# Relative-position rows of 800 bytes in a decoder layer's self-attention, their constant end filled on chip, and 72 queries turned in every tile

## The chip, the cores and the metric

One core of one Trainium2 chip runs the whole program in one launch. The metric is device time in microseconds (us).

## What is computed

A decoder layer in float32 on x of 4 x 1024 x 256: self-attention with relative positions, cross-attention to a context of 4 x 154 x 256, and a gated feed-forward with quantised activations and weights, each followed by a residual sum and a layer norm. The change is in the self-attention, with 16 heads of 16:

```python
attn = jnp.einsum('bhld,bhrd->bhlr', q, k) * scale
dist = jnp.clip(jnp.arange(L)[None, :] - jnp.arange(L)[:, None], -LEFT, RIGHT) + LEFT   # LEFT, RIGHT = 64, 8
rel = jnp.einsum('bhld,lrd->bhlr', q, dist_emb[dist]) * scale
out = jnp.einsum('bhlr,bhrd->bhld', jax.nn.softmax(attn + rel, axis=-1), v)
```

A query's relative term is constant for all keys more than 64 to the left and for all keys at least 8 to the right. Only a band of 72 positions differs from key to key. The kernel subtracts the right constant everywhere, so that the right end is zero.

## The kernel before

**Tiles.** The attention works in 32 tiles T (NT). A tile is four heads (G) and half a sequence of queries, 512 (HALF); two tiles in a row, even and odd T, are the two halves of the same four heads. In a tile, kt runs over eight blocks of 128 keys. For each kt and head, `scores` forms scores with keys on the partitions and 512 queries in the columns (`scoresT`, L851 and L856), ACT takes the exponential (L604), and `weigh` multiplies with the values (L869). Besides, 16 chunks a tile (`max_chunk`, L822 and L823, one tile and a half ahead) form the same scores with queries on the partitions, and DVE finds each query's maximum in them (L696 to L701), which becomes a shift per query.

**The band.** `make_row(T, j)` (L796) multiplies 128 queries of four heads with the 72 embeddings; ACT copies the result into `rows` at column LP = 184 (L581); POOL fills the 184 columns to the left with the row's first value, the left constant (`pad_row`, L478); SP stores the 256 columns of 1024 bytes in `rel_table` in DRAM (`store_row`, L323), where each row has 128 more columns of zeros, cleared once in the opening (L339). SP reads a window back with a row pitch that is one element shorter (`load_windows`, L315), so that row p is shifted by p: `win` holds for each query block the 256 columns that lie over the key block to its left and over its own. Column c of row p is the left constant where c < 56 + p, the band up to 128 + p, and zero behind it. There are four row stores and four window loads for each tile, 512 KB each.

**Turning.** A score block needs the window with keys on the partitions. `scores` therefore adds it with a matmul that turns it: the window is the stationary operand, the identity the moving one (L856). The left constant of far keys comes with the main product instead, by three more rows of operands (102 in place of 99) for the columns from `cut` on. `side` is the place of the query block behind kt within the tile. For side 0, 1 and 2 only the first 72 queries (SIDE) of that block are turned, and the product has two pieces with `cut` between them:

```python
side = (kt + 1) % TL - 4 * hf
...
elif 0 <= side < 3:
    cut = side * P + SIDE
else:
    cut = min(max((side + 1) * P, 0), HALF)
```

For side 3 (kt = 2 in an even tile, kt = 6 in an odd one) the product is one piece of 512 columns with 99 rows, and all 128 queries of the block are turned.

**Shift.** POOL forms the shift of a tile (`shift_of`, L493 to L500) from the left constant in `win[..., 0]` and DVE's maxima, cuts a window's wrapped end to zero (`cut_window`, L484), PE turns the shift at kt = 5 (`turn_shift`, L804), ACT copies it (L587) and SP places it in the query operand with four DMAs (`place_shift`, L328). The next tile's first score waits for it.

**Order.** Each engine's program is written out by hand in one order. The opening runs projections of eight blocks of 512 rows in 48 steps, and between them the rows of tiles 0 to 2 and the first 24 chunks. SP issues every load and store of the attention in one queue, in the order of the code: `load_windows(0)` waits for the four row stores of tile 0 to land, `load_q(1)` follows it, and `load_windows(1)` follows the row stores of tile 1. In the loop over tiles SP stores row block 3 of tile T + 3 at kt = 4, then the attention's output, then places the shift at kt = 5. POOL's order in a tile is: two row copies, the normalisation, one row copy, the shift, the cut, one row copy.

Of the kernel before, what the change touches and what calls it, by code (L numbers as in the profile page):

```python
# [9 lines left out]
ALU = mybir.AluOpType  # L10
# [3 lines left out]
P = 128  # L14
# [5 lines left out]
G = 4  # L20
# [25 lines left out]
def self_attention(nc, sem, ad, xT, wqT, wkT, wvT, bq, bk, bv, emb, part_of_row, e_lo, e_hi, ident,  # L46
# [9 lines left out]
    LP = 184  # L56
    NC = LP + NJ
    TWID = NC + P
    WID = 2 * P
    VW = HD + 1  # L60
# [7 lines left out]
    with ctx:  # L68
# [63 lines left out]
        w_cut = sem("w_cut")  # L132
        m_left = sem("m_left")
# [107 lines left out]
        def _(sp):  # L241
# [67 lines left out]
            def load_windows(T):  # L309
                for j in range(4):  # L310
                    sp.wait_ge(st_row[j], 16 * (T + 1))
                for h in range(G):
                    first = ((T % 2 * G + h) * HALF) * TWID + P
                    src = bass.AP(tab.tensor, first, [[TWID - 1, P], [P * TWID, 4], [1, WID]])
                    sp.dma_start(win[:, T % NW, :, h, :], src).then_inc(ld_w[T % NW], 16)  # L315
# [21 lines left out]
            for r in range(2):  # L337
                for h in range(G):
                    sp.dma_start(tab[r, h].rearrange("(t p) n -> p t n", p=P)[:, :, NC:TWID],  # L339
                                 zero[:, :].rearrange("p (t n) -> p t n", n=P)).then_inc(s_pads, 16)  # L340
# [30 lines left out]
            sp.wait_ge(s_pads, 16 * 2 * G)  # L371
# [79 lines left out]
        def _(pool):  # L451
# [28 lines left out]
            def cut_window(T):  # L480

                pool.wait_ge(m_top, T + 1)
                cut = win[:, T % NW, 0, :, 0:P - WRAP] if T % 2 == 0 else win[:, T % NW, 3, :, WID - WRAP:WID]
                nc.gpsimd.memset(cut, 0.0).then_inc(w_cut, 1)  # L484

            def shift_of(T):

                w = win[:, T % NW, :, :, 0]
# [11 lines left out]
                nc.gpsimd.tensor_tensor(parts[2], rest, parts[1], ALU.subtract).then_inc(m_ready, 1)  # L500

# [9 lines left out]
            for k, n in steps:  # L511
# [9 lines left out]
                if (k, n) == (6, 4):  # L521
                    shift_of(0)
                    cut_window(0)
            for T in range(NT):
# [10 lines left out]
                if T + 1 < NT:  # L535
                    shift_of(T + 1)
                    cut_window(T + 1)
# [103 lines left out]
        def _(dve):  # L641
# [40 lines left out]
            def chunk(T, c):  # L682
# [20 lines left out]
                if c == CH - 1:  # L703
                    dve.wait_ge(x_read, n + 1)
                    nc.vector.tensor_tensor(mx[:, T % 2, :, :, 3], mx[:, T % 2, :, :, 0], win[:, T % NW, :, :, 0], ALU.add).then_inc(m_left, 1)
# [50 lines left out]
        def _(pe):  # L756
# [69 lines left out]
            def scores(T, kt, h):  # L826
                i, hf = T // 2, T % 2
                if kt == 0 and h == 0:
                    pe.wait_ge(sh_in[hf], 16 * G * (i + 1))
                    pe.wait_ge(ld_k[i % 2], 16 * 4 * (i // 2 + 1))  # L830
                    pe.wait_ge(ld_w[T % NW], 16 * G * (T // NW + 1))
                if kt == TL - 1 and h == 0:
                    pe.wait_ge(w_cut, T + 1)
# [8 lines left out]
                elif 0 <= side < 3:  # L842
# [1209 lines left out]
```

## Time and profile before

| what | value |
|---|---|
| median of 3 runs | 1430.61 us (1427.94 to 1431.42) |
| the profiled execution: its own time | 1430.84 us |
| the profiled execution: span, first to last instruction | 1429.0 us |
| mean granted clock of TensorE | 0.947 |
| PE busy | 1258.5 us, 88% |
| DVE busy | 1056.4 us, 74% |
| ACT busy | 974.0 us, 68% |
| POOL busy | 346.8 us, 24% |
| DMA, mean over the span | 191 GB/s |

PE is TensorE's matmuls, PEld its weight loads, DVE is VectorE, ACT ScalarE, POOL GpSimd, SP the engine whose queue issues the DMAs (SPq). L and a number is a line of the kernel. In the first 128 us the opening runs, the tiles of self-attention follow to about 960 us, then cross-attention and, from 1116 us, the feed-forward part. A clock of 1.00 is 2.4 GHz, 0.5 is 1.2 GHz.

### The profile page before, as it was taken

To read this page: it belongs to the slowest core of one execution; us is meant where nothing else is said; L and a number is where in the kernel's file an instruction comes from. 1 tells how busy PE (TensorE), PEld (TensorE's weight loads), DVE (VectorE), ACT (ScalarE), POOL (GpSimd) and SP (SyncE) were. 2 spreads that over 40 slices of the span, in tenths; PEclk is the share of its full clock that TensorE was granted. 3 is DMA by queue.
4 is the path that set the end of the run, shared out by engine and by line. 5 is a ranking of instruction groups with operands and counts; after the bars stand their busy time and mean duration, and the time that the engine had idled before them with its cause. 6 is when DMAs were issued, how large, how long until landed. Compare 5 with 4: busy or idle time off the path is not lost. (4 is left out here: it accounts for less than half of the span.)

```text
span 1429.0 us, 25354 instructions
## 1 busy us (share of the span) xinstructions
PE 1258.5 (88%) x8412; PEld 671.9 (47%) x8412; DVE 1056.4 (74%) x2561; ACT 974.0 (68%) x1690; POOL 346.8 (24%) x573
## 2 busy tenths in 40 slices
PE   8787999999999999999999999999997799910596
PEld 4343344334334334334434433437885687710586
DVE  4376788888887888888888888862574457999676
ACT  4434777777777777777777777773665558959661
POOL 4544121211211211212112121004552002420022
PEclk9989999999999999999999999999998899965798
DMA  8999977878888788697797786625321313825033
GB/s 251 303 335 259 252 210 224 227 206 244 225 220 228 214 244 219 195 266 214 208 252 211 227 226 183 211 75 166 97 75 45 133 59 119 315 84 217 1 104 103
DMA packets 263759, 273.14 MB, mean 191 GB/s; under 512 B 66222, under 2 KB 246990, under 8 KB 259534
## 3 DMA queue, kind: packets, MB, share of 16 engines
q1 hardware_dynamic: 261998, 268.39, 64.5%
q10 hardware_dynamic: 1632, 3.15, 0.7%
q8 instruction: 67, 1.10, 0.3%
q14 instruction: 62, 0.51, 0.1%
HBM read 153.69 MB, written 117.00 MB: 189 GB/s over the span
## 5 line engine op out<-in xcount | busy, mean ns | idle before, releaser
L604 ACT ACTIVATE pr<-scoresT 128x512 f32<-128x512 f32 x1024 | 548.1, 601 | 212.1 <-PE scoresT L856 151.9
L851 PE MATMUL scoresT<-qT,kT 99*128 99x512 bf16 (+7 forms) x1408 | 356.6, 327 | 6.0 <-DVE attn_out L741 2.3
L701 DVE TENSOR_REDUCE mx<-scores_for_max 128x1 f32<-128x888 f32 (+6 forms) x448 | 301.6, 673 | 0.0
L696 DVE CUSTOM_DVE_ANT_0 junk<-scores_for_max,win 128x200 f32<-128x200 f32 (+2 forms) x512 | 179.9, 351 | 159.1 <-PE scores_for_max L823 149.5
L699 DVE TENSOR_REDUCE mx<-scores_for_max 128x1 f32<-128x64 f32 (+6 forms) x448 | 277.4, 619 | 0.0
L869 PE MATMUL attn_out<-pr,vS 128*17 128x512 f32 x2048 | 271.2, 602 | 6.5 <-DMA vS<-v_all 6.3
L851 PEld LDWEIGHTS scoresT<-qT,kT 99*128 99x128 bf16 (+1 forms) x1408 | 107.4, 97 | 335.1 <-ACT rows L581 97.8
L856 PE MATMUL scoresT<-idf,win 128*128 128x128 f32 (+1 forms) x1024 | 200.7, 257 | 0.0
L478 POOL COPY rows<-rows 128x736 f32<-128x736 f32 x128 | 102.2, 798 | 381.2 <-ACT rows L581 381.2
L822 PE MATMUL scores_for_max<-kX,qT 64*128 64x512 bf16 x512 | 167.2, 384 | 4.0 <-DVE mx L701 3.0
L823 PE MATMUL scores_for_max<-kX,qX 64*128 64x512 bf16 x512 | 167.2, 384 | 0.0
L856 PEld LDWEIGHTS scoresT<-idf,win 128*128 128x128 f32 (+1 forms) x1024 | 137.4, 142 | 17.4 <-issue 0.6
L1977 PE MATMUL banks<-w_gate_high,x_high 128*128 128x256 f32 x128 | 37.6, 294 | 90.4 <-DVE x_low L1902 90.4
L1846 DVE TENSOR_REDUCE amax<-raw 128x1 f32<-128x3072 f32 (+2 forms) x26 | 80.6, 3099 | 5.9 <-ACT raw L1749 5.6
L822 PEld LDWEIGHTS scores_for_max<-kX,qT 64*128 64x128 bf16 x512 | 35.9, 94 | 102.7 <-issue 52.5
L1977 PEld LDWEIGHTS banks<-w_gate_high,x_high 128*128 128x128 f32 x128 | 25.4, 199 | 92.1 <-issue 84.3
L581 ACT ACTIVATE rows<-scoresT 128x288 f32<-128x288 f32 x128 | 54.5, 426 | 11.1 <-DMA rel_table<-rows 10.4
L1749 ACT ACTIVATE raw<-banks,step 128x512 f32<-128x512 f32 x48 | 33.0, 688 | 29.3 <-PE banks L1952 29.3
L796 PE MATMUL scoresT<-embS,qT 96*128 96x72 bf16 x512 | 37.8, 196 | 17.1 <-DMA qT<-q_parts 11.2
L869 PEld LDWEIGHTS attn_out<-pr,vS 128*17 128x17 f32 x2048 | 34.2, 96 | 39.0 <-issue 11.5
L468 POOL TENSOR_TENSOR shared<-rem,shared 128x512 bf16<-128x512 f32 x32 | 36.8, 1155 | 57.1 <-ACT shared L557 56.9
L507 POOL TENSOR_TENSOR shared<-ov,orec 128x256 f32<-128x256 f32 x16 | 9.9, 622 | 147.0 <-PE scoresT L851 104.6
(216 smaller groups left out, 1977.4 us busy)
## 6 DMA issues: line engine op xcount, KB each, us to landing
rel_table<-rows SPq DMA_DIRECT2D x128, 512.0 KB, 4.5
win<-rel_table SPq DMA_DIRECT2D x128, 512.0 KB, 5.4
up_raw<-xT_normed SPq DMA_DIRECT2D x6, 1536.0 KB, 10.0
xT_normed<-up_raw SPq DMA_DIRECT2D x6, 1536.0 KB, 6.6
qT<-q_parts SPq DMA_DIRECT2D x32, 256.0 KB, 7.5
kX<-k_parts SPq DMA_DIRECT2D x64, 128.0 KB, 4.9
kT<-k_parts SPq DMA_DIRECT2D x32, 256.0 KB, 5.6
q_parts<-shared SPq DMA_DIRECT2D x32, 192.0 KB, 4.5
```

The source lines that it names most:

```text
L478: nc.gpsimd.tensor_copy(rows[:, j, :, 0:LP], rows[:, j, :, LP:LP + 1].to_broadcast([P, G, LP])).then_inc(r_padded, 1)
L604: nc.scalar.activation(pr[:, n % NPR, h, :], bank, ACT.Exp).then_inc(t_read, 1)
L696: last = nc.vector.tensor_tensor_reduce(junk[:, n % 2, 0:z - a], bank[:, a:z], win[:, T % NW, q4, h, u:u + z - a], 1.0, NEG, ALU.add, ALU. ...
L699: last = nc.vector.tensor_reduce(mx[:, T % 2, q4, h, 0:1], bank[:, 0:a], AX.X, ALU.max)
L701: last = nc.vector.tensor_reduce(mx[:, T % 2, q4, h, 2:3], bank[:, z:L], AX.X, ALU.max)
L822: mm(psX[:, n % 2, 0:HALF], qT[0:64, q_slot(i), h, lo:lo + P], kX[0:64, i % 2, h, :], start=True, stop=True)
L823: mm(psX[:, n % 2, HALF:L], qX[64:128, i % 2, h, lo:lo + P], kX[64:128, i % 2, h, :], start=True, stop=True).then_inc(x_full, 1)
L851: last = mm(bank[:, a:e], k[0:r], q[0:r, a:e], start=(n == 0), stop=not near and n == len(pieces) - 1, skip_group_check=True)
L856: last = mm(bank[:, a:e], rel, idf[0:e - a, 0:e - a], is_transpose=True, start=False, stop=n == len(near) - 1, skip_group_check=True)
L869: last = mm(psO[32 * h:32 * h + VW, :], vS[:, i % 2, kt, VW * h:VW * (h + 1)], pr[:, n % NPR, h, :], start=(kt == 0), stop=(kt == TL - 1))
L1846: nc.vector.tensor_reduce(amax[:, k, n:n + 1], src, AX.X, ALU.max, apply_absolute_value=True).then_inc(done, 1)
L1977: mm(to(n, q), oh[m // 2][:, c], wdh[:, d], start=(m == 0 and q % 2 == 0), stop=False, skip_group_check=True)
```

## The change

1. LP falls from 184 to 128: a row is 200 columns, 800 bytes. A table row is 328 columns. The window load brings 200 columns, into columns 56 to 255 of `win` (FLAT = 56). The columns 0 to 55, which are the left constant in every row, are no longer loaded.
2. A new POOL step `fill_ends` behind `shift_of` writes columns 0 to 55 from column 56, for 72 partitions and all 16 blocks. `scores` waits for it (`w_flat`) at a tile's first product, `cut_window` too. Readers of the left constant read column 56.
3. The end columns are cleared by row groups of 32 partitions for all heads and blocks together, 128, 96, 64 and 32 columns wide, as far as a shifted row can reach.
4. `side` 3 is treated as sides 0 to 2.

```diff
-    LP = 184
+    LP = 128
     NC = LP + NJ
     TWID = NC + P
     WID = 2 * P
+    ENDS = 4
+    FLAT = P - LEFT - WRAP
...
-                    src = bass.AP(tab.tensor, first, [[TWID - 1, P], [P * TWID, 4], [1, WID]])
-                    sp.dma_start(win[:, T % NW, :, h, :], src).then_inc(ld_w[T % NW], 16)
+                    src = bass.AP(tab.tensor, first, [[TWID - 1, P], [P * TWID, 4], [1, WID - FLAT]])
+                    sp.dma_start(win[:, T % NW, :, h, FLAT:WID], src).then_inc(ld_w[T % NW], 16)
...
             for r in range(2):
-                for h in range(G):
-                    sp.dma_start(tab[r, h].rearrange("(t p) n -> p t n", p=P)[:, :, NC:TWID],
-                                 zero[:, :].rearrange("p (t n) -> p t n", n=P)).then_inc(s_pads, 16)
+                for part_ in range(ENDS):
+                    rows_ = slice(part_ * P // ENDS, (part_ + 1) * P // ENDS)
+                    width = P - rows_.start
+                    dst = tab[r].rearrange("h (t p) n -> p (h t) n", p=P)[rows_, :, NC:NC + width]
+                    sp.dma_start(dst, zero[rows_, 0:width].unsqueeze(1).to_broadcast([P // ENDS, 4 * G, width])).then_inc(s_pads, 16)
...
                 pool.wait_ge(m_top, T + 1)
+                pool.wait_ge(w_flat, T + 1)
...
-                w = win[:, T % NW, :, :, 0]
+                w = win[:, T % NW, :, :, FLAT]
...
+            def fill_ends(T):
+
+                ends = win[0:SIDE, T % NW].rearrange("p q h n -> p (q h) n")
+                nc.gpsimd.tensor_copy(ends[:, :, 0:FLAT], ends[:, :, FLAT:FLAT + 1].to_broadcast([SIDE, 16, FLAT])).then_inc(w_flat, 1)
...
                 if T + 1 < NT:
                     shift_of(T + 1)
+                    fill_ends(T + 1)
                     cut_window(T + 1)
...
                     pe.wait_ge(ld_w[T % NW], 16 * G * (T // NW + 1))
+                    pe.wait_ge(w_flat, T + 1)
...
-                elif 0 <= side < 3:
+                elif 0 <= side < 4:
                     cut = side * P + SIDE
```

On PE, in tile 0 at kt = 2 (side 3), two heads stand in the order before like this, with the main product (L851) and the turned windows (L856):

```order
L851 MATMUL scoresT<-qT,kT 128x512
L856 MATMUL scoresT<-idf,win 128x128 x2
L851 MATMUL scoresT<-qT,kT 128x512
L856 MATMUL scoresT<-idf,win 128x128 x2
L851 MATMUL scoresT<-qT,kT 128x512
L856 MATMUL scoresT<-idf,win 128x128 x2
```

and like this in the changed kernel, where the lines are L866 and L871:

```order
L866 MATMUL scoresT<-qT,kT 128x456
L866 MATMUL scoresT<-qT,kT 128x56
L871 MATMUL scoresT<-idf,win 128x128
L871 MATMUL scoresT<-idf,win 128x72
L866 MATMUL scoresT<-qT,kT 128x456
L866 MATMUL scoresT<-qT,kT 128x56
L871 MATMUL scoresT<-idf,win 128x128
L871 MATMUL scoresT<-idf,win 128x72
```

A head there has four matmuls in place of three, 712 columns in place of 768; nothing else on PE moved.

On POOL, within one tile of the loop, the row copies (L478), the normalisation (L507), the shift (L493 to L500) and the cut (L484) stand before like this:

```order
L478 COPY rows<-rows 128x4x184 [waits t_read]
L493 TENSOR_SCALAR shift_of<-win 128x16 [waits ld_w1]
L497 CAST mcol<-shift_of 128x2x4x4 [waits t_full,m_top,m_small]
L498 TENSOR_TENSOR shift_rem<-shift_of,mcol 128x32 [waits m_small]
L499 CAST mcol<-shift_rem 128x2x4x4 [waits m_small]
L500 TENSOR_TENSOR mcol<-shift_rem,mcol 128x2x4x4 [waits m_small]
L484 MEMSET win 128x4x120 [waits m_top]
L478 COPY rows<-rows 128x4x184 [waits t_read] x3
```

and now, with the fill as L512 and the other lines 7 further down:

```order
L484 COPY rows<-rows 128x4x128 [waits t_read]
L500 TENSOR_SCALAR shift_of<-win 128x16 [waits ld_w1]
L504 CAST mcol<-shift_of 128x2x4x4 [waits t_full,m_top,m_small]
L505 TENSOR_TENSOR shift_rem<-shift_of,mcol 128x32 [waits m_small]
L506 CAST mcol<-shift_rem 128x2x4x4 [waits m_small]
L507 TENSOR_TENSOR mcol<-shift_rem,mcol 128x2x4x4 [waits m_small]
L512 COPY win<-win 72x16x56
L491 MEMSET win 128x4x120 [waits w_flat,m_top]
L484 COPY rows<-rows 128x4x128 [waits t_read] x3
```

The fill came in between the shift and the cut, so the tile's fourth row copy, the first of the last row, stands one operation later.

On SP, the clearing of the end columns was eight issues of the form `128x4x128`, and is now twice the following four:

```order
L345 DMA rel_table<-zero 32x16x128 [waits s_zero]
L345 DMA rel_table<-zero 32x16x96
L345 DMA rel_table<-zero 32x16x64
L345 DMA rel_table<-zero 32x16x32
```

The number of issues and of pieces is as before, and the stores of the queries' parts follow behind them as they did.

## Rows read from the trace of the kernel before

**Rows 1.** The page, busy time of each engine and its share of the span.
```profile
PE 1258.5 (88%) x8412; PEld 671.9 (47%) x8412; DVE 1056.4 (74%) x2561; ACT 974.0 (68%) x1690; POOL 346.8 (24%) x573
```
**Rows 2.** Busy time by stretch: from:to, length, engines, clock, DMA share, GB/s.
```profile
62.00:76.00 14.00, 4.18 (x14) 1.39 (x13) 4.53 (x9) 3.51 (x6) 4.16 (x5) 0.78 0.96 284
76.00:127.00 51.00, 50.11 (x180) 24.05 (x177) 38.59 (x101) 23.21 (x40) 29.34 (x33) 0.96 0.98 304
127.00:142.00 15.00, 6.95 (x56) 3.75 (x56) 6.39 (x19) 4.84 (x10) 2.27 (x3) 0.87 1.09 289
400.00:600.00 200.00, 197.67 (x1515) 80.67 (x1512) 165.46 (x487) 152.15 (x303) 42.35 (x88) 1.00 0.83 229
```
**Rows 3.** Waits of PE, 212 to 960: who for whom, total us, times, longest.
```profile
PE scoresT L796 <- ACT pr L604: 4.2, 13, 0.4
PE scores_for_max L822 <- DVE mx L701: 3.0, 13, 0.6
```
**Rows 4.** Timeline of PE, kt 5 and 6 of an odd tile: start us, us, operation.
```profile
492.19 0.40 PE L851 MATMUL scoresT<-qT,kT 99*128 99x328 bf16 x2
...
492.60 0.39 PE L851 MATMUL scoresT<-qT,kT 99*128 99x328 bf16 x2
...
495.74 0.39 PE L851 MATMUL scoresT<-qT,kT 99*128 99x512 bf16 x1
...
496.19 0.38 PE L851 MATMUL scoresT<-qT,kT 99*128 99x512 bf16 x1
```
**Rows 5.** Timeline inside one head: a turned window, and the next one's weight load.
```profile
495.97 0.27 PE L856 MATMUL scoresT<-idf,win 128*128 128x128 f32 x1
...
495.97 0.14 PEld L856 LDWEIGHTS scoresT<-idf,win 128*128 128x128 f32 x1
```
**Rows 6.** Timeline of weight loads where PE had waited: turning, and float32 of a projection.
```profile
1030.07 0.14 PEld L1446 LDWEIGHTS banks<-idf,at 128*128 128x128 f32 x1 [0.70 <-issue]
...
1030.07 0.20 PEld L1446 LDWEIGHTS banks<-idf,at 128*128 128x128 f32 x2 [0.70 <-issue]
...
83.15 0.19 PEld L779 LDWEIGHTS attn_out<-wv,xs 128*128 128x128 f32 x1 [0.23 <-issue]
...
83.15 0.30 PEld L779 LDWEIGHTS attn_out<-wv,xs 128*128 128x128 f32 x2 [0.23 <-issue]
```
**Rows 7.** Busy time by stretch: end columns, then values, then windows flow.
```profile
10.50:14.50 4.00, 4.00 (x10) 1.72 (x10) 1.53 (x3) 2.52 (x5) 1.70 (x2) 1.00 1.05 285
137.50:138.50 1.00, 0.00 (x0) 0.00 (x0) 0.00 (x0) 0.00 (x0) 0.00 (x0) 0.85 1.24 105
505.00:507.00 2.00, 2.00 (x20) 1.05 (x12) 1.76 (x6) 1.28 (x4) 0.80 (x1) 1.00 1.09 386
```
**Rows 8.** Waits of SP's queue, 0 to 230.
```profile
SPq L311 <- DMA rel_table<-rows: 8.1, 7, 1.3
```
**Rows 9.** Timeline of SP: first and second windows, first values.
```profile
62.10 2.49 SPq L315 DMA_DIRECT2D win<-rel_table  x4
...
83.21 2.48 SPq L315 DMA_DIRECT2D win<-rel_table  x4
...
132.11 0.38 SPq L307 DMA_DIRECT2D vS<-v_all  x1
```
**Rows 10.** Timeline of PE: the two waits for a transfer.
```profile
75.81 0.42 PE L796 MATMUL scoresT<-embS,qT 96*128 96x72 bf16 x4 [9.82 <-DMA qT<-q_parts]
...
140.31 1.91 PE L869 MATMUL attn_out<-pr,vS 128*17 128x512 f32 x8 [6.33 <-DMA vS<-v_all]
```
**Rows 11.** The page, costliest groups: POOL's row copy and its normalisation.
```profile
L478 POOL COPY rows<-rows 128x736 f32<-128x736 f32 x128 | 102.2, 798 | 381.2 <-ACT rows L581 381.2
...
L507 POOL TENSOR_TENSOR shared<-ov,orec 128x256 f32<-128x256 f32 x16 | 9.9, 622 | 147.0 <-PE scoresT L851 104.6
```
**Rows 12.** Timeline, SP and PE around the start of tile 15.
```profile
521.93 0.36 SPq L323 DMA_DIRECT2D rel_table<-rows  x1
...
524.48 1.36 SPq L328 DMA_DIRECT2D qT<-sh  x2
...
528.20 0.39 PE L851 MATMUL scoresT<-qT,kT 102*128 102x512 bf16 x1
```

More of the change, by code:

```diff
@@ L132, in self_attention @@
         w_cut = sem("w_cut")
+        w_flat = sem("w_flat")
         m_left = sem("m_left")
@@ L370, in _ @@
             store_parts(3, 1)
-            sp.wait_ge(s_pads, 16 * 2 * G)
+            sp.wait_ge(s_pads, 16 * 2 * ENDS)
             load_windows(0)
@@ L522, in _ @@
                     shift_of(0)
+                    fill_ends(0)
                     cut_window(0)
@@ L704, in chunk @@
                     dve.wait_ge(x_read, n + 1)
-                    nc.vector.tensor_tensor(mx[:, T % 2, :, :, 3], mx[:, T % 2, :, :, 0], win[:, T % NW, :, :, 0], ALU.add).then_inc(m_left, 1)
+                    nc.vector.tensor_tensor(mx[:, T % 2, :, :, 3], mx[:, T % 2, :, :, 0], win[:, T % NW, :, :, FLAT], ALU.add).then_inc(m_left, 1)
                     if T:
```

## The prediction

> **What bounds the kernel now.** I read the page's engine times first, then the busy time by stretch, then the waits, then the timeline around the places that the change touches. PE is busy 88% of the span [rows 1], and the stretches say how that average is made up [rows 2]: between 400 and 600 us PE is busy 197.7 of 200 us at a granted clock of 1.00 (2.4 GHz), with DVE at 165 and ACT at 152; the 32 tiles of the attention run like this from 128 to about 960 us. From 62 to 76 us PE is busy only 4.2 of 14 us and the DMA share is 0.96; from 127 to 142 us it is 7 of 15 us with the DMA share over 1. Between them, 76 to 127 us, PE is full again. Between 212 and 960 us PE itself waits for 4.2 and 3.0 us in its two largest groups [rows 3], none of them a DMA. So there are two currencies: in the tiles only PE's own instructions count, and in the opening it is the two holes in which PE waits for a transfer. The feed-forward part behind 1116 us is not touched.
>
> **Part 1, 72 queries turned in all tiles (PE).** One key step in each tile (side 3: kt 2 of an even tile, kt 6 of an odd one) had per head one product of 512 columns and two turned windows of 128; it gets products of 456 and 56 columns and turned windows of 128 and 72, the form of the two steps ahead of it. The timeline gives both forms one behind the other [rows 4]: the step with pieces 328 and 184 and windows 128 and 72 starts its heads 0.41 us apart, the one to be changed 0.45 us. The ends differ by 0.04 us a head, over 4 heads x 32 tiles = 128 heads: 5.1 us, if the new form costs what its neighbours cost. I do not think it does. A weight load starts when the product before it starts and not earlier: the load for the second window stands at 495.97, with the first window's start [rows 5]. What such a load takes is seen where PE had been waiting: the first turning load at 1030.07 lasts 0.14 in the record, two of them 0.20 together, so the second starts 0.06 us behind the first [rows 6]. In the neighbours the piece ahead of the first window has 184 or 312 columns, and by the 512 columns that take 0.23 us (495.74 to 495.97 [rows 4, 5]) that is at least 0.08 us, which covers 0.06. The new piece of 56 columns takes 0.03 and leaves 0.03 open. So a head comes to 0.405 + 0.028, against 0.444: 0.011 less, x128 = **1.4 us less**. Bounds: nothing is left open, 5.1 less; or the load takes all of the 0.08 that the 184 columns hide, then 0.055 is open, 0.015 more a head, 1.9 us more. I take the load's own row, because it is the same instruction form.
>
> The Trainium skill, page "TensorE: Matmul & The Clock Gate", section "LDWEIGHTS (loading the stationary operand)", says that a load takes its columns / 1.2 ns, 107 ns for 128. The trace agrees for a float32 load that doesn't turn: two at 83.15 take 0.30 with 0.19 for one, so 0.11 apart [rows 6]; for the turning ones it disagrees, with 0.06. By the page's figure 0.08 us would be open a head and the sum would be 1432. A load of that length is a rival below.
>
> **Part 2, rows of 800 bytes (DMA).** A row store of one query block and a window load of one head each move 2048/4 = 512 packets of 1024 bytes; a set of four is 2048 packets. Where windows alone flow (505 to 507 us) they come at 386 GB/s; where the 512-byte end columns flow (10.5 to 14.5 us) it is 285 GB/s [rows 7]. Over 16 engines that is 42.4 and 28.7 ns a packet, and linearly between them 36.4 ns for 800 bytes. A set shrinks from 5.4 to 4.65 us: 0.77 less. Bounds: in proportion to the bytes, 1.2 less; nothing; or worse than nothing, since 800 is no multiple of 64 and every second row now starts in the middle of 64 bytes. The nearest row for that is the value load with its 272-byte pieces, which flow alone from 137.5 to 138.5 us at 105 GB/s [rows 7], 41 ns a packet where the line through 512 and 1024 gives 22: about 20 ns more. A set would then take 2.6 us more than I count, 1.8 more than now.
>
> In the tiles this buys nothing: no PE wait there names a DMA. In the opening it does. SP waits for the first row stores to land (8.1 us in 7 waits [rows 8]) and issues the first windows at 62.10; the queries of the next heads are queued behind them, and PE waits for those 9.82 us, until 75.81 [rows 9, 10]. In front of that landing lie one set of rows and one of windows: 2 x 0.77 = **1.5 us less** (0 to 2.4). The second windows go out at 83.21, again when rows have landed, and from there SP issues without a pause worth naming until the values at 132.11 [rows 9], for which PE waits 6.33 us, until 140.31 [rows 10]. On that way lie two more sets of rows and two of windows, 3.1 us, but part of SP's time there is pure issuing, about 0.6 us an issue, which no smaller packet shortens. I count two thirds, **2.0 us less** (up to 4, and the other way by the bound above). The hole can't give more than its 6.33 us.
>
> **Part 3, end columns cleared in four parts.** Eight issues stay eight and 4096 packets stay 4096, of 512, 384, 256 and 128 bytes. They flow around 10 to 17 us, and PE's first hole behind them is at 62. I cost it at nothing; its cover is the 45 us until the first window load needs them.
>
> **Part 4, the constant filled by GpSimd.** POOL's copies of a row fall from 736 to 512 elements; at 798 ns for 736 [rows 11] that is 0.24 less for each of four a tile. The fill has 16 x 56 = 896 elements, 0.97 us by the same price. POOL's sum stays the same, but the order doesn't: the fill stands behind the shift and ahead of the fourth row copy. SP stores that row (521.93) and behind it sends the shift (last of four issues at 525.2, from the two that fill 524.48 to 525.84), which the next tile's first product at 528.20 needs [rows 12]. The row copy ends 0.97 - 0.24 - 0.24 = 0.5 us later, and so does the shift. From the last issue to the product are 3.0 us, and a small transfer needs at most some 2.1 (the shortest landing in the list of transfers, as an estimate): 0.9 us of slack take 0.5. **Nothing** on the path. The new wait of PE for the fill is met some 7 us ahead.
>
> **Sum** against the profiled execution (1430.84 us; span 1429.0): -1.4 - 1.5 - 2.0 = -4.9, 1425.9. The median of the runs shown, 1430.61, is the same within 0.2, so 1426.
>
> **Rivals.**
> A. The new heads cost what the neighbours cost. For it: no row shows a turning load behind a piece this short, so that nothing in the tiles contradicts it. Against: the load's 0.06 us of its own [rows 6]. Then part 1 gives 5.1: 1430.8 - 5.1 - 3.5 = 1422.2.
> B. The opening gives nothing: packets cost what they cost, or SP's issuing sets all. For: the 0.6 us issues behind 83.21. Against: the saturated DMA share [rows 2]. 1430.8 - 1.4 = 1429.4.
> C. GpSimd delays the shift. Its price may be that of a two-input operation over 16 runs, 622 ns for 256 elements [rows 11], 2.4 ns each: 2.18 us. The shift is then 1.7 late, 0.8 past the slack, in some 15 odd tiles (an even tile has about 2 us): +12. 1430.8 - 4.9 + 12 = 1438, slower than before. It decides from a fill of 1.4 us. Against it: memory copies have the other price in this trace.
> D. Packets of 800 bytes pay the 20 ns of the 272-byte ones: 1.8 us more than now for each of the two sets ahead of 76 us and for two thirds of the four behind, +8.4 in the opening. In a tile eight such transfers take 3.6 us more of 26, and the DMA share goes from 0.83 to 0.97, still beside PE. 1430.8 - 1.4 + 8.4 = 1438. For: the alignment. Against: windows start at any multiple of 4 bytes already and still flow at full rate.
> E. The window's load takes as long as the float32 load of the projection at 83.15, 0.11 us [rows 6]: 0.08 open, +5 from part 1 in place of -1.4: 1432. Against: the 184-column piece shows no gap.
> F. The change doesn't do what it says, for instance because both holes are refilled by other transfers: 1430, about B.
>
> **How the numbers follow.** A measurement of this kernel can tell about 0.3%, 4.3 us, from no change. The forecast has 0.46, and its own spread (1422 to 1429) lies around 1426.5, so 0.29 of it counts as faster and 0.17 as the same; A 0.18, all faster; B and F together 0.24, nearly all the same, 0.02 of it faster by a shorter stretch at the low clock behind the holes; C 0.04, D 0.05, E 0.03, of which 0.08 slower and 0.04 the same. That gives 0.49 faster, 0.43 the same, 0.08 slower. The range of 8 in 10 runs from A with the full 2.4 and 4 us of the opening (1419) to just above B (1431.5), and leaves out C and D.
>
> **What would show it.** PE: heads of the changed step 0.43 apart, with the first window's start 0.06 behind the 56-column piece (0.03 for A, 0.11 for E). The waits that end at 75.81 and 140.31 end at about 74.3 and 136.8. Window loads flow at 350 GB/s or more, and a set takes 4.65 us. POOL's fill lasts 0.97 us and the shift's last issue moves by 0.5 without a PE wait. I am wrong if a tile pair's period grows, if PE waits for the shift, or if PE's two holes close at their old times.

## The result and the profile after

| | before | changed |
|---|---|---|
| median | 1430.71 us (14 runs, 1427.94 to 1433.83) | 1427.82 us (14 runs, 1425.13 to 1430.79) |
| the profiled execution: own time, span | 1430.84, 1429.0 us | 1425.76, 1424.0 us |
| mean granted clock of TensorE | 0.947 | 0.948 |
| DMA, mean over the span | 191 GB/s | 171 GB/s |
| POOL busy | 346.8 us | 353.8 us |

The ratio of changed to before is 0.9971, with a 95% interval of 0.9963 to 0.9980: 4.1 us less, between 2.9 and 5.3. (The two medians in the table are 2.9 apart; where this document speaks of microseconds under before, it is by the ratio.) The forecast was 1426.0 us.

The busy time by stretch of the changed kernel (columns as in [rows 2]):

```profile
62.00:76.00 14.00, 5.13 (x14) 1.55 (x12) 3.85 (x9) 4.35 (x8) 3.87 (x5) 0.84 0.91 248
76.00:127.00 51.00, 50.47 (x180) 24.31 (x180) 38.53 (x99) 22.77 (x40) 29.63 (x33) 0.94 1.02 301
127.00:142.00 15.00, 10.53 (x74) 6.19 (x72) 7.13 (x21) 7.04 (x14) 2.51 (x4) 0.81 1.12 267
400.00:600.00 200.00, 197.67 (x1539) 80.67 (x1536) 165.51 (x487) 152.18 (x303) 43.34 (x95) 1.00 0.74 188
```

Against [rows 2], PE has gained 3.6 us of work between 127 and 142 us and less than one between 62 and 76. In the steady stretch it is as busy as before, while the DMA share fell from 0.83 to 0.74 and the flow from 229 to 188 GB/s, which changes nothing for PE there. The same two waits for a transfer as in [rows 10], timeline of PE:

```profile
76.53 0.42 PE L810 MATMUL scoresT<-embS,qT 96*128 96x72 bf16 x4 [9.40 <-DMA qT<-q_parts]
...
138.31 1.05 PE L884 MATMUL attn_out<-pr,vS 128*17 128x512 f32 x8 [2.00 <-DMA vS<-v_all]
```

The first wait ends 0.7 us later than before and is 0.4 us shorter, the second ends 2.0 us earlier and has shrunk from 6.33 to 2.00 us. The end of a tile is marked by ACT's copy of the tile's sum (`ot<-attn_out`). Tile 1 and tile 31, before:

```profile
195.25 0.59 ACT L608 ACTIVATE ot<-attn_out 128x512 f32<-128x512 f32 x1
...
964.01 0.60 ACT L608 ACTIVATE ot<-attn_out 128x512 f32<-128x512 f32 x1 [1.17 <-PE attn_out L869]
```

and changed:

```profile
191.51 0.59 ACT L622 ACTIVATE ot<-attn_out 128x512 f32<-128x512 f32 x1
...
958.34 0.60 ACT L622 ACTIVATE ot<-attn_out 128x512 f32<-128x512 f32 x1 [1.17 <-PE attn_out L884]
```

So this pair of executions is 3.7 us apart at the end of the opening, and the 30 tiles between the marks take 766.83 us in place of 768.76, 1.9 less. Behind the tiles 0.6 us are lost again. The experiments are read by these "30 tiles". They repeat within a few hundredths where PE does not wait for the shift (766.83 and 766.86 in the changed kernel and e1_old_ends, 762.83, 762.85 and 762.83 in e4_swap, e9_q_first and e10_q2_late), but only within 0.3 us in the kernel before, whose tiles e2_four_parts leaves as they are (768.76 and 769.07). The opening differs by 1 to 2 us between executions of like kernels, so there I read groups of runs, and the part behind the tiles takes from 464.4 to 467.5 us in the thirteen profiled executions, though no edit touches it.

### The profile page after: what moved, and what is told of

It reads as the page before. It is cut to its first block and busy times, and to the rows that moved or that the text cites. A ratio compares the mean times of both kernels' runs of the same rounds, so it can differ in the third digit from the quotient of the medians.

```text
span 1424.0 us, 25674 instructions
## 1 busy us (share of the span) xinstructions
PE 1257.3 (88%) x8540; PEld 673.5 (47%) x8540; DVE 1057.2 (74%) x2561; ACT 974.3 (68%) x1690; POOL 353.8 (25%) x605
## 5 line engine op out<-in xcount | busy, mean ns | idle before, releaser
L866 PE MATMUL scoresT<-qT,kT 99*128 99x512 bf16 (+9 forms) x1536 | 356.9, 313 | 6.1 <-issue 2.3
L866 PEld LDWEIGHTS scoresT<-qT,kT 99*128 99x128 bf16 (+1 forms) x1536 | 113.3, 98 | 334.0 <-ACT rows L595 97.0
L871 PE MATMUL scoresT<-idf,win 128*128 128x128 f32 (+1 forms) x1024 | 199.3, 256 | 0.0
L484 POOL COPY rows<-rows 128x512 f32<-128x512 f32 x128 | 78.6, 614 | 361.0 <-ACT rows L595 361.0
L871 PEld LDWEIGHTS scoresT<-idf,win 128*128 128x128 f32 (+1 forms) x1024 | 127.8, 143 | 19.2 <-issue 0.7
L836 PEld LDWEIGHTS scores_for_max<-kX,qT 64*128 64x128 bf16 x512 | 36.0, 93 | 100.8 <-issue 47.5
L595 ACT ACTIVATE rows<-scoresT 128x288 f32<-128x288 f32 x128 | 54.2, 423 | 11.4 <-DMA rel_table<-rows 10.6
```

The source lines that it names most:

```text
L484: nc.gpsimd.tensor_copy(rows[:, j, :, 0:LP], rows[:, j, :, LP:LP + 1].to_broadcast([P, G, LP])).then_inc(r_padded, 1)
L836: mm(psX[:, n % 2, 0:HALF], qT[0:64, q_slot(i), h, lo:lo + P], kX[0:64, i % 2, h, :], start=True, stop=True)
L866: last = mm(bank[:, a:e], k[0:r], q[0:r, a:e], start=(n == 0), stop=not near and n == len(pieces) - 1, skip_group_check=True)
L871: last = mm(bank[:, a:e], rel, idf[0:e - a, 0:e - a], is_transpose=True, start=False, stop=n == len(near) - 1, skip_group_check=True)
```

## The experiments

All medians are beside runs of the kernel before on the same chip; the last column is the length of the 30 tiles in the profiled execution.

| kernel | median, us (runs) | before, us | ratio, 95% interval | 30 tiles, us |
|---|---|---|---|---|
| changed | 1427.82 (14) | 1430.71 | 0.9971, 0.9963 to 0.9980 | 766.83 |
| e1_old_ends | 1426.16 (5) | 1431.61 | 0.9960, 0.9946 to 0.9974 | 766.86 |
| e2_four_parts | 1432.66 (11) | 1431.61 | 0.9998, 0.9987 to 1.0010 | 769.07 |
| e3_turns | 1432.05 (11) | 1431.61 | 1.0002, 0.9993 to 1.0011 | 768.36 |
| e4_swap | 1422.82 (5) | 1431.61 | 0.9938, 0.9925 to 0.9951 | 762.83 |
| e5_pad_behind | 1431.63 (12) | 1431.27 | 1.0007, 0.9995 to 1.0019 | 768.17 |
| e6_no_turns | 1428.75 (11) | 1430.65 | 0.9987, 0.9977 to 0.9998 | 768.34 |
| e7_wide | 1430.02 (12) | 1431.27 | 0.9985, 0.9974 to 0.9996 | 766.97 |
| e8_v_first | 1424.97 (6) | 1431.27 | 0.9949, 0.9934 to 0.9964 | 763.82 |
| e9_q_first | 1421.55 (5) | 1431.27 | 0.9926, 0.9912 to 0.9940 | 762.85 |
| e10_q2_late | 1418.66 (5) | 1430.65 | 0.9915, 0.9901 to 0.9929 | 762.83 |
| e11_all | 1419.83 (5) | 1430.65 | 0.9912, 0.9896 to 0.9928 | 764.15 |

### The end columns, each way (e1_old_ends, e2_four_parts)

The first is the changed kernel with the old clearing, the second the kernel before with the new one:

```diff
-                for part_ in range(ENDS):
...
+                for h in range(G):
+                    sp.dma_start(tab[r, h].rearrange("(t p) n -> p t n", p=P)[:, :, NC:TWID],
+                                 zero[:, :].rearrange("p (t n) -> p t n", n=P)).then_inc(s_pads, 16)
```

> The changed kernel with the end columns of the table cleared as before (eight DMAs of one head each, 128 columns wide), everything else as changed. In the changed kernel SP spends 7.0 us on the eight four-part clearings where it spent 6.0 us on the old ones, and the first store of projected parts starts 1.0 us later. Theory 1 (the clearing is on the path that opens the kernel): the stores, the row stores and the first windows come 1 us earlier, and the time is about 1 us below the changed kernel, 1426.8. Theory 2 (the prediction's: the clearing costs nothing, the late opening of the changed kernel is a run's own phase): the time is that of the changed kernel within 0.4 us, and the first hole of PE ends at the same time.

> The kernel before with the four-part clearing alone (widths 128, 96, 64 and 32 columns, both head sets in one DMA). Theory 1: SP's issue of the eight takes 7.0 us in place of 6.0, and the time is about 1 us over the kernel before, 1431.7. Theory 2: the time is that of the kernel before within 0.4 us.

The timeline of SP's queue, changed kernel:

```profile
8.66 6.99 SPq L345 DMA_DIRECT2D rel_table<-zero  x8
...
15.70 1.34 SPq L268 DMA_DIRECT2D q_parts<-shared  x2
```

and e1_old_ends:

```profile
8.45 6.00 SPq L342 DMA_DIRECT2D rel_table<-zero  x8
...
15.10 2.22 SPq L268 DMA_DIRECT2D q_parts<-shared  x3
```

The eight issues do take 1.0 us more of SP in the new form. The time doesn't show it: e2_four_parts is at 0.9998, and e1_old_ends lies 0.11% under the changed kernel's ratio, less than the intervals can tell. PE's first wait ended at 77.85 in e2_four_parts and at 77.20 in e1_old_ends, inside the 75.8 to 78.1 of all kernels up to e8_v_first. Theory 2 is nearer, but a cost of up to about 1 us stays possible.

### The turns alone (e3_turns)

```diff
-                elif 0 <= side < 3:
+                elif 0 <= side < 4:
```

> The kernel before with the one edit that 72 queries are turned in the fourth tile too (side < 4), rows of 1024 bytes and no fill. Theory 1 (from the two traces: the head of the changed step takes 0.438 us in place of 0.4437, 128 heads): 0.8 us less than before, 1429.9, and the 128-wide window still starts 0.03 us late behind the piece of 56 columns. Theory 2 (the prediction's 11 ns a head): 1.4 us less, 1429.3. Theory 3 (the head costs what its neighbours cost, 0.405): 5 us less, 1425.6.

The time is that of before: theory 3 is out, and the interval, up to 1.0 us less, excludes theory 2 as well. The 30 tiles are 0.40 us shorter than before, and 0.71 shorter than in e2_four_parts, whose tiles are those of before. A head of the changed step, from the first product of one head to the next one's, takes 0.438 us in e3_turns and in the changed kernel, where it took 0.444. That is 0.7 us over 128 heads, theory 1. Beside the kernel before every odd tile is 0.02 us shorter and the even tiles are not: their starts, laid beside those of before instruction by instruction, lead by 0.02 us until kt = 5, and not behind PE's turning of the shift. What stands there is in the view of that line (212 to 960 us), before:

```profile
L804 PEld LDWEIGHTS scoresT<-minus_ident,mcol x112: 94/98/100, 234.7 to 935.1; 128*128 128x128 bf16 x112
...
  POOL mcol L500: 3.7, 15
```

and e3_turns:

```profile
L804 PEld LDWEIGHTS scoresT<-minus_ident,mcol x112: 95/98/99, 234.2 to 934.2; 128*128 128x128 bf16 x112
...
its engine sat idle before it (us, times) until:
  POOL mcol L500: 4.0, 15
```

The weight load waits 0.2 to 0.3 us for POOL in each even tile, which leaves PE about 0.08 short. It looks as if PE waited away what it had gained, but e2_four_parts, which gained nothing, has the same waits in its view of that line (L808 there):

```profile
  POOL mcol L504: 4.0, 15
```

POOL's work ahead of the shift begins with the normalisation, and that is released by PE. From a tile's start mark it stands at 11.273 us before and in e2_four_parts and at 11.255 in e3_turns (medians of the even tiles 6 to 24): PE's lead is handed on. The shift is ready at 14.307 before, at 14.326 in e2_four_parts and at 14.309 in e3_turns, so it is POOL's stretch between that was 0.02 us shorter in the one profiled execution of before. Beside e2_four_parts the even tiles of e3_turns keep their 0.02 us too.

### Which side of the change gave the even tiles their tenth (e5_pad_behind)

In the changed kernel an even tile is 0.10 us shorter, an odd one 0.02. The same view of the changed kernel:

```profile
L818 PEld LDWEIGHTS scoresT<-minus_ident,mcol x112: 95/96/100, 230.8 to 929.4; 128*128 128x128 bf16 x112
...
its engine sat idle before it (us, times) until:
  POOL mcol L507: 1.0, 2
```

Thirteen waits for the shift are gone. POOL's row copy ahead of the shift takes 614 ns in place of the 798 of [rows 11] (costliest groups of the page):

```profile
L484 POOL COPY rows<-rows 128x512 f32<-128x512 f32 x128 | 78.6, 614 | 361.0 <-ACT rows L595 361.0
```

e5_pad_behind gives the kernel before the same head start in another way:

```diff
-                if T + 3 < NT:
-                    pad_row(T + 3, 2)
                 if T + 1 < NT:
                     shift_of(T + 1)
+                if T + 3 < NT:
+                    pad_row(T + 3, 2)
+                if T + 1 < NT:
                     cut_window(T + 1)
```

> The kernel before with one step moved on GpSimd: the fill of the third row tile (0.80 us) behind the shift of the next tile instead of ahead of it. Theory (the changed kernel's even tiles gain 0.10 us each where its odd ones gain 0.02, because the shift comes 0.18 us earlier behind a shorter fill, and PE's turning of the shift had waited some 0.08 us for it): PE's even tiles become 0.10 us shorter here too, 16 of them 1.5 us, odd ones stay, and the time is about 1.5 us under the kernel before. Rival (the even tiles' gain is the turned windows' or the DMA flow's): both kinds of tile stay as they are, 0.00 a tile, and the time is that of the kernel before within 0.4 us.

The waits fell to the same 1.0 us, 2 times, and at kt = 5 of an even tile PE led by 0.075 us, as the theory has it. But the time did not move, and the 30 tiles gained 0.59, not 1.2: in some tiles the fill that now comes late delayed the row store and the shift queued behind it on SP, and PE waited again at the next tile (0.1 us in tile 12; once 0.3 us for `qT<-sh`). So the cause of the even tiles' gain is confirmed, and this way to get it is no gain: the 1.5 us that I had expected did not come (1.0007, 0.7 us less to 2.7 more).

### The windows' packets (e7_wide) and the rows without the turns (e6_no_turns)

e7_wide is e1_old_ends with windows of 1024-byte rows (GpSimd writes the constant over the extra 56 columns):

```diff
-                    first = ((T % 2 * G + h) * HALF) * TWID + P
-                    src = bass.AP(tab.tensor, first, [[TWID - 1, P], [P * TWID, 4], [1, WID - FLAT]])
-                    sp.dma_start(win[:, T % NW, :, h, FLAT:WID], src).then_inc(ld_w[T % NW], 16)
+                    first = ((T % 2 * G + h) * HALF) * TWID + P - FLAT
+                    src = bass.AP(tab.tensor, first, [[TWID - 1, P], [P * TWID, 4], [1, WID]])
+                    sp.dma_start(win[:, T % NW, :, h, :], src).then_inc(ld_w[T % NW], 16)
```

> The changed kernel with windows of 1024-byte rows: the first 56 columns are loaded too and GpSimd then fills the constant over them. The stored rows, their shorter copies and fills and the turns stay as changed, and the end columns are cleared as before. Theory 1 (the opening's gain is the windows' packets): a set of windows takes 0.9 us longer in each of the three sets ahead of the values, so that the values land 1.7 to 3 us later and PE's products of the first values start near 141 in place of 138.4; time 2 to 3 us over the changed kernel, 1430 to 1431. Theory 2 (the gain is the shorter row stores and the shorter fills on GpSimd): the products start near 138.4 and the time stays within 0.6 us of the changed kernel. In both the steady tiles keep their length, within 0.02 us.

e6_no_turns is the changed kernel with `side < 3` and the fill over 128 partitions in place of 72:

> The changed kernel without its edit of the turned queries (side < 3 as before, the constant filled over all 128 rows), so rows of 800 bytes alone. Theory: the opening is the changed kernel's (PE's products of the first values start near 138.4), the even tiles are as in the changed kernel or up to 0.02 us longer, the odd tiles 0.02 us longer each, and the time is 0.4 to 0.8 us over the changed kernel. Rival (the turns bear the tiles' gain): the even tiles lose their 0.10 us again and the time is 1.9 us over the changed kernel.

PE's first products of the values in e7_wide:

```profile
142.33 1.91 PE L881 MATMUL attn_out<-pr,vS 128*17 128x512 f32 x8 [6.44 <-DMA vS<-v_all]
```

and in e6_no_turns:

```profile
138.66 1.05 PE L884 MATMUL attn_out<-pr,vS 128*17 128x512 f32 x8 [2.67 <-DMA vS<-v_all]
```

Theory 1 holds, in time too (2.1 us under before, where the changed kernel is 4.1 under). With 1024-byte windows these products start at 140.31, 142.29, 141.70, 142.56 and 142.33 us (before, e2, e3, e5, e7), with 800-byte windows at 138.31, 138.48, 138.37 and 138.66 (changed, e1, e4, e6): means 141.84 and 138.46, 3.4 us apart, without an overlap. e7_wide has short rows, short fills and the turns, and still stands in the first group; its time is 0.25% over e1_old_ends. It is the only run that parts the windows from the rows, with one profiled execution. Its 30 tiles are the changed kernel's within 0.14 us, so the steady gain is not the windows'. The issues of SP say where the 3.4 us arise. From the first issue of the first windows to that of the second windows it takes 21.1 to 21.4 us with 1024-byte windows (e7_wide 21.36) and 20.6 to 20.8 with 800-byte ones; from there to the values 47.5 to 48.9 us (e7_wide 48.35) and 45.5 to 46.1. The rows, short or long, make no difference in either stretch, nor in front of it: the first windows are issued at 62.10, 63.73, 63.69 and 63.40 us with rows of 1024 bytes (before, e2, e3, e5), and at 63.25, 64.01, 63.48, 62.93 and 64.02 with rows of 800 (changed, e1, e4, e6, e7). The page says how long each transfer takes to land, e7_wide:

```profile
win<-rel_table SPq DMA_DIRECT2D x128, 512.0 KB, 5.4
rel_table<-rows SPq DMA_DIRECT2D x128, 400.0 KB, 4.9
```

and changed:

```profile
rel_table<-rows SPq DMA_DIRECT2D x128, 400.0 KB, 4.1
win<-rel_table SPq DMA_DIRECT2D x128, 400.0 KB, 5.0
```

A row store of 400 KB lands in 4.1 us beside windows of 800 bytes and in 4.9 beside windows of 1024, where one of 512 KB takes 4.5 to 4.8 (before, e2, e3, e5).

e6_no_turns opens like the changed kernel and keeps the even tiles' gain (its view of the turned shift also says 1.0, 2). Its 30 tiles are 0.4 us under before; one of them, tile 6, was 0.63 longer, where PE waited once, 0.7 us, for `qT<-sh`. Without that the 30 tiles are 1.1 under before. Its time is 1.9 us under before (0.3 to 3.3), which lies nearer to the rival's price than to the theory's: it is the tiles that speak for the theory, not the time.

### The order of the two pieces (e4_swap)

```diff
                 pieces = [(a, e, r) for a, e, r in ((0, cut, KR + 3), (cut, HALF, KR + 6)) if a < e]
+                if side == 3:
+                    pieces.reverse()
```

> The changed kernel with the two pieces of the scores in the fourth tile issued the other way round: the 56 columns first, then the 456. If the 31 ns before the turned window are the load of its 128 float32 columns, which needs cover and has only the 56 columns' 0.03 us, then 456 columns cover it: the head of that step falls from 0.438 to 0.405 us, 128 heads give 4.2 us, and the time is about 1423.6. Rival (the load waits for another thing, as the change from bf16 to float32 operands, whatever stands ahead of it): the 31 ns stay, the head is 0.43 to 0.44, and the time stays within 0.4 us of the changed kernel's 1427.8.

Timeline of PE inside kt = 6 of tile 13, changed kernel:

```profile
491.19 0.39 PE L866 MATMUL scoresT<-qT,kT 99*128 99x456 bf16 x2
491.42 0.37 PE L871 MATMUL scoresT<-idf,win 128*128 128x128 f32 x2
491.63 0.39 PE L866 MATMUL scoresT<-qT,kT 99*128 99x456 bf16 x2
```

and e4_swap:

```profile
491.25 0.39 PE L868 MATMUL scoresT<-qT,kT 102*128 102x56 bf16 x2
491.49 0.34 PE L873 MATMUL scoresT<-idf,win 128*128 128x128 f32 x2
491.66 0.38 PE L868 MATMUL scoresT<-qT,kT 102*128 102x56 bf16 x2
```

The pair of turned windows takes 0.37 us where the 56 columns stand right ahead of it and 0.34 where the 456 do; the heads start 0.44 and 0.41 us apart. Within the pair, the second window starts 0.142 to 0.144 us behind the first in the changed kernel and 0.110 to 0.112 in e4_swap. Over 128 heads 0.033 us is 4.2; the 30 tiles went from 766.83 to 762.83, 4.0 less, and the time is 8.9 us under before (7.0 to 10.7). The rival is out: the load of the float32 window needs cover, and that is all the 0.03 us were. The second window, of 72 rows, has the first one ahead of it in both orders.

### The opening as one flow (e8_v_first to e11_all)

e8_v_first and e9_q_first are e4_swap with one move each on SP: `load_max_operands(1)` from behind `load_windows(2)` to behind `load_v(0)`; and

```diff
+            load_q(1)
             sp.wait_ge(s_pads, 16 * 2 * ENDS)
             load_windows(0)
-            load_q(1)
```

> The changed kernel with the swapped pieces, and the load of the second head group's operands for the maximum (seven DMAs, 5 us of flow) moved behind the load of the first values. PE waits 1.2 to 2.0 us for those values. Theory: they land 4 us earlier, the wait is gone, and the time is 1.5 us under that of the swapped pieces alone, about 1421.3. Rival (something else is late next: the exponentials or the score banks): the wait moves and at most 0.5 us is gained.

> The changed kernel with the swapped pieces, and the load of the second group's queries (four DMAs) moved ahead of the first windows on SP. Theory 1 (the first hole is set by what lands last, the queries, 3.3 us behind the windows, and the fourth window shares its time with them): the queries land some 8 us earlier, the windows about 1 us earlier, PE goes on near 75.5 in place of 76.8, and the time is about 1 us under that of the swapped pieces alone, 1421.8. Theory 2 (the flow is full throughout, so the windows land as much later as the queries take): VectorE's first maximum, and behind it the remainder that PE waits for, start 2 us later, and the time is 0.5 to 2 us over it, 1423.3 to 1424.8.

e8_v_first took the wait for the values down to 0.77 us and gave it back: tile 1's shift became late, so that it is the rival's case, and the time is no shorter than that of e4_swap. Timeline of PE, e4_swap:

```profile
161.31 1.15 PE L868 MATMUL scoresT<-qT,kT 102*128 102x512 bf16 x3 [3.73 <-DMA qT<-sh]
```

and e8_v_first:

```profile
162.35 1.46 PE L868 MATMUL scoresT<-qT,kT 102*128 102x512 bf16 x3 [7.92 <-DMA qT<-sh]
```

This third hole is in every run so far, before too (1.78 us, until 163.64), and no sentence of mine had it. e9_q_first moved the opening: PE's first hole now ends at 74.94, with another cause.

```profile
73.58 0.30 DVE L710 CUSTOM_DVE_ANT_0 junk<-scores_for_max,win 128x136 f32<-128x136 f32 x1 [8.48 <-DMA win<-rel_table]
...
74.94 0.60 PE L836 MATMUL scores_for_max<-kX,qT 64*128 64x512 bf16 x1 [6.94 <-DVE mx L715]
```

What PE waits for now is DVE behind the windows. The other two kernels with this order (e10_q2_late and e11_all, below) start that maximum at 74.96 and 73.83, and PE goes on at 76.32 and 75.19. So with the queries ahead of the windows the maximum starts at 74.1 us in the mean of three, against 73.1 in the five kernels with 800-byte windows and the old order (changed, e1, e4, e6, e8), and PE goes on at 75.5 against 76.6. The windows do land later, by 1.0 us, half of what theory 2 said, and PE still goes on 1.1 us earlier, as theory 1 said; the longer time of theory 2 did not come. The ends of tile 1 stand at 193.07 in e4_swap and 190.97 here, and the time is 10.6 us under before (8.6 to 12.6).

e10_q2_late is e9_q_first with the third group's queries behind the first `place_shift` of the loop:

```diff
-                        if i + 2 < NIT:
+                        if T and i + 2 < NIT:
                             load_q(i + 2)
...
                         place_shift(T + 1)
+                        if T == 0:
+                            load_q(2)
```

> As the kernel with the queries ahead of the first windows (swapped pieces, 800-byte rows), and the load of the third group's queries (four DMAs, some 4 us of flow) moved from step 1 of tile 0 to behind the shift of tile 1. PE waits at tile 1's first 102-row product for that shift in every run (1.0 to 7.9 us), 5 to 6 us behind its issue. Theory (the shift lies in the flow behind those queries): it lands some 3 us earlier, PE's tile 1 starts 2 us earlier, and the time is about 2 us under the kernel with the queries first, 1419.5. Rival (the queries now come late for the row products of tile 4, at 165 us): the wait moves there and the time stays within 0.5 us.

> The kernel of e10_q2_late with the operands for the maximum behind the first values as well. Alone, that move had taken away the wait for the values and given the time back at tile 1's shift. Theory (all three are one flow, and what PE waits for last sets the start of tile 1): with the third group's queries out of the way the 3.7 us wait for the values goes too, and the time is 1 to 2.5 us under that of e10_q2_late. Rival (the shift of tile 1 is bound by the maxima on VectorE, which start no earlier): the wait for it grows by what the wait for the values loses, and the time is that of e10_q2_late within 0.5 us.

In e10_q2_late no wait for the shift of tile 1 is left; the next one is the rival's, for the moved load:

```profile
159.86 0.42 PE L812 MATMUL scoresT<-embS,qT 96*128 96x72 bf16 x4 [2.31 <-DMA qT<-q_parts]
```

By the trace it is 1.2 us ahead of e9_q_first at the end of tile 0 and 0.2 at the end of tile 1. Its ratio is lower by 0.0011, which the intervals can't tell apart. In e11_all PE no longer waits for the values, but the wait for the shift is back with 4.04 us, until 156.02. Its tile 1 ends 1.3 us ahead of e10_q2_late, and this lead is gone by tile 31 (both at 953.6). It goes in four tiles, 4, 14, 16 and 24, which are 0.79, 0.13, 0.21 and 0.17 us longer than in e10_q2_late, in each of them at the first product that needs the next tile's shift. Timeline of PE, e11_all, end of tile 4:

```profile
262.88 0.82 PE L870 MATMUL scoresT<-qT,kT 102*128 102x512 bf16 x3 [0.73 <-DMA qT<-sh]
```

So the 1 to 2.5 us of the theory did not come either. e10_q2_late is the best version run that I would keep: 12.2 us under before (10.2 to 14.2), and under the changed kernel too.

## Why the prediction was right, point by point

The forecast of 1426.0 lies 1.8 us under the median, and the measured 4.1 us less beside my 4.9. The sum hides two terms that missed and one that was not there, and that it came out so close is in part luck.

**Part 1, the turns: the mechanism was right, the term mis-sized.** I had a head at 0.405 + 0.028 = 0.433 us and 1.4 us in all. The gap is there, with 31 ns, and e4_swap shows by taking it away that it is the window's load without cover. It does not stand where I had said: the record has the first window's start 0.03 us behind the 56-column piece, which was my sign for rival A, and the 31 ns behind that start, ahead of the second window. Only the length of the head tells the two apart, and it is 0.438: 5 ns of error against a difference of 11. The step that missed is therefore a difference of nearly equal numbers, 0.7 us in place of 1.4. Rival A is excluded by the head of 0.438, rival E also: 0.11 of load would have opened 0.08.

The page of the Trainium skill "TensorE: Matmul & The Clock Gate", section "LDWEIGHTS (loading the stationary operand)", says that a load takes its columns / 1.2 ns. An estimate from its 107 ns for 128 columns, less the 0.03 us of the 56 columns, opens 0.08 us a head; for this load the trace disagrees, with 0.03.

**Part 2, the rows: the sum right, its terms wrong.** I had 1.5 us in the first hole and 2.0 in the second, from shorter row stores and shorter windows alike, 0.77 a set. In the groups of runs the first wait ends at 77.3 (1024-byte windows) and 76.7 (800), 0.6 apart, and by the first score nothing of it is left (129.97 and 129.92); the second ends 3.4 us earlier. Two steps missed.

The first is that a set of row stores gives what a set of windows gives. It gave nothing: the first windows are issued no earlier behind rows of 800 bytes, and e7_wide, with short rows and long windows, stands with the 1024-byte group throughout. That is why the first hole gave 0.6 and not 1.5: only the windows' own term came, from their issue to the end of PE's wait 13.9 us in the mean with 1024-byte windows and 13.2 with 800. That is about the 0.77 of one set. The flow of windows in the changed kernel, 2.5 us behind their issue as in [rows 7]:

```profile
499.40:501.40 2.00, 2.00 (x21) 0.92 (x20) 1.86 (x7) 1.38 (x3) 0.29 (x1) 1.00 1.10 342
```

By 342 and 386 GB/s a set shrinks by 0.6 us, where my line through two packet sizes had 0.77 (and at least 350 GB/s).

The second is "two thirds" for the second hole. By my price the two sets of windows there were worth 1.0 us; they gave 2.7 between the issue of the second windows and that of the first values, after 0.5 in the stretch ahead of it. Part of that is in SP's issuing itself: from the second windows to the second store of values behind them (`v_all<-vs`, at 98.52 in e1_old_ends and 100.79 in e7_wide) it took 13.9 us with short windows and 15.4 with long ones. So the queue there was paced by what had to land, though hardly a wait of it was worth naming. Why the windows are worth that much in it stays open. A term too many and a term too small thus made 3.5 us beside a measured 3.4. Rivals B and F are out by the second hole, rival D too: nothing was paid for windows of 800 bytes, and nothing seen for rows of 800 bytes.

**Part 3, the end columns.** Costed at nothing, with no cost found (up to about 1 us could hide in the noise), but the new form takes SP 1.0 us longer, which I had not seen: eight issues are not eight equal issues.

**Part 4, GpSimd: nothing on the path of the changed kernel's trace, and a gain that I had missed.** The fill:

```profile
L512 POOL COPY win<-win x32: 927/928/931, 115.1 to 929.2; 72x896 f32<-72x896 f32 x32
```

0.93 us against my 0.97, far from rival C's 1.4. But the shorter row copy gives 0.18 us (798 to 614 ns), not 0.24, and POOL is busy 7 us more in all, where I had the same. Timeline, start of an odd tile, changed kernel:

```profile
519.00 2.95 SPq L331 DMA_DIRECT2D qT<-sh  x4
...
523.53 0.82 PE L866 MATMUL scoresT<-qT,kT 102*128 102x512 bf16 x3
```

From the first issue of the shift to the product that needs it are 4.5 us; before, 5.3 (522.89 to 528.20). So 0.8 of the slack went, not 0.5. In the profiled execution of the changed kernel it held. It is thin, though: with the fill in the same place the longest wait of PE for the shift in the tiles was 0.7 us in e6_no_turns, 0.6 in e8_v_first and 0.7 in e11_all, and in the traces of before, e2_four_parts and e3_turns it had none. Whether these late landings are owed to the 0.8 us no run shows. What I had missed lies at the other end: the shorter copy ahead of the shift brings the shift earlier, by which the even tiles gained about 0.08 us each, 1.2 to 1.3 in all, more than the turns. I had read the waits of PE's products, of which [rows 3] shows the two largest; in the full list of them POOL stands once, with 0.4 us. The view of the line that turns the shift counts the waits of the weight loads too, and there they are 15, 3.7 us.

**The account.** Opening 3.4 (groups of runs), the shift 1.2, the turns 0.7: 5.3, at the upper end of the measured 2.9 to 5.3. The part behind the tiles, untouched, differs by 0.6 us between the two profiled executions and by about 3 us among all of them, so the times can't check this sum more closely than their interval.

## What to carry to other kernels

A turned float32 window needs something ahead of it on PE (with 56 columns there each head cost 0.03 us more than with 456): where a product has two pieces, put the long piece directly in front of it and the short one first. When an edit shortens a transfer in an opening where the flow is full, follow the queue to every wait behind it, and expect that what you take from one hole is partly waited in the next, as in e8_v_first and e11_all. Check each kind of transfer by itself before you count it: here the windows gave all of the opening's gain and the row stores none. Read the waits of the weight loads as well as those of the products. And before a few hundredths of a microsecond a tile are explained, look at how far two executions with the same tiles lie apart: 0.02 us a tile here.

## What the runs showed that I had not expected

- A wait of a weight load for POOL of 0.2 us, in each second tile, cost 0.08 us of PE there (3.7 us, 15 times before; 1.0 us, 2 times after), and of the products' waits only one, of 0.4 us, names POOL.
- Eight clearing DMAs with 4096 packets in all take SP 6.00 us to issue when each has 128 x 4 rows of 512 bytes, and 6.99 us when each has 32 x 16 rows of 512 to 128 bytes.
- Rows of 800 bytes, whose start in DRAM is not a multiple of 64 bytes in every second row, showed no extra cost, and as stores they gained nothing of their own: a window of 400 KB lands in 4.9 to 5.0 us where one of 512 KB takes 5.4, but a row store of 400 KB takes 4.1 beside the short windows and 4.9 beside the long ones (e7_wide).
- Putting four loads of queries ahead of the first windows, with a DMA share of 0.9 in that stretch (0.91 in the changed kernel), made DVE's first use of the windows later by 1.0 us in the mean (74.1 against 73.1 us), and PE went on 1.1 us earlier all the same.
